# The attention mask moved from matmuls to accumulating transfers, and the row biases to GpSimd and ScalarE

## What is computed

```python
x = rotate_pairs(x, theta[b], phi[b])
h = gelu(x @ Wi[e] + bi[e]); x = ln(x + h @ Wo[e] + bo[e]) * gamma[e] + beta[e]      # e = expert of b, 256 -> 1024 -> 256
out = gelu(x @ w1 + b1) @ w2 + b2                                                   # c = 0, 1: "narrow"
out = gelu(gelu(x @ w1_sr + b1_sr) @ w2_sr + b2_sr) @ w3_sr + b3_sr                 # c = 2: "deep", 256 -> 512 -> 256 -> 256
x = ln(x + out) * gamma2 + beta2
x = adaptive_ln(x, timestep[b])
scores = q @ k.T / 4 + fside[b, head];  scores[mask[b]] = -inf                      # 16 heads of 16 columns
x = x + (softmax(scores) @ v) @ Wo + bo
x = x + gelu2(ln(x) * g2 + beta2 @ W1 + b1) @ W2 + b2                               # gelu2(h) = h * sigmoid(1.702 h)
```

## Time and profile before

| | before |
|---|---|
| three runs | 2249.8, 2251.36, 2251.6 us (median 2251.36) |
| the profiled execution, its own time | 2250.72 us |
| its span | 2248.9 us |
| TensorE busy | 2024.3 us, 90% |
| VectorE busy | 1563.6 us, 70% |
| ScalarE busy | 1314.8 us, 58% |
| GpSimd busy | 122.6 us, 5% |
| share of the 16 DMA engines taken by SyncE's queue | 50.3% |

### The profile page before, as it was taken

How to read it: one execution, slowest core, us unless ns; L and a number is a source line. 1 busy time by engine, 2 the same in 40 slices (tenths; PEclk the granted TensorE clock), 3 DMA queues, 4 the chain that set the end, 5 groups by cost and what they waited for, 6 DMA issues and landing times.

```text
span 2248.9 us, 43734 instructions
## 1 busy us (share of the span) xinstructions
PE 2024.3 (90%) x14735; PEld 1739.7 (77%) x14735; DVE 1563.6 (70%) x5410; ACT 1314.8 (58%) x2086; POOL 122.6 (5%) x268
## 2 busy tenths in 40 slices
PE   4488999999999999999999999999999999998986
PEld 3467788888878888878788777888787788877865
DVE  4357777777776677776776777766777767777763
ACT  3256566656556666556666656665665666565632
POOL 1000000000000000000000000000000000000000
PEclk8689999999999999999999999999999999999998
DMA  5355554555455455555554455455555545554440
GB/s 195 101 158 158 166 155 141 168 180 161 148 167 151 146 175 162 166 166 151 145 168 157 153 158 181 139 159 171 170 159 168 171 128 170 176 163 144 124 137 24
DMA packets 217606, 347.52 MB, mean 155 GB/s; under 512 B 29139, under 2 KB 115443, under 8 KB 217364
## 3 DMA queue, kind: packets, MB, share of 16 engines
q1 hardware_dynamic: 217364, 344.37, 50.3%
HBM read 285.51 MB, written 58.79 MB: 153 GB/s over the span
## 4 chain that ended last, share of the span: by engine, by line
PE 62%; DVE 11%; DMA 9%; SPq 6%; issue 6%; ACT 5%; DVEq 0%; ACTq 0%; POOL 0%; POOLq 0%
PE pD L425 41%; DMA out<-res 8%; PE pX L640 8%; PE pS L425 7%; SPq L267 5%; DVE x_scores L1131 3%; PE pC L425 3%; PE pD L430 2%; ACT gelu_out L737 2%; DVE x_scores L917 2%; DVE res L920 2%; ACT hid L737 1%; PE pC L660 1%; DVE res L914 1%; DVE xc_lo L914 1%
## 5 line engine op out<-in xcount | busy, mean ns | idle before, releaser
L1131 DVE CUSTOM_DVE_ANT_0 x_scores<-pS,bias_ring 128x256 f32<-128x256 f32 x1024 | 390.8, 419 | 221.6 <-PE pS L425 207.5
L737 ACT ACT_TABLE_LOAD x347 | 445.2, 1283 | 34.7 <-PE pD L425 28.1
L737 ACT ACTIVATE probs<-pX 128x512 f32<-128x512 f32 x512 | 304.8, 595 | 257.1 <-PE pX L640 252.3
L640 PE MATMUL pX<-ident,x_scores 128*128 128x128 f32 x2048 | 326.9, 283 | 60.2 <-DVE x_scores L917 58.4
L640 PEld LDWEIGHTS pX<-ident,x_scores 128*128 128x128 f32 x2048 | 237.7, 143 | 129.6 <-DVE x_scores L917 97.8
L917 DVE TENSOR_SCALAR x_scores<-x_scores,row_max 128x256 f32<-128x256 f32 x1024 | 315.5, 351 | 18.3
L425 PE MATMUL pS<-k_stack,q_stack 96*128 96x256 f32 x1024 | 306.1, 381 | 0.0
L425 PE MATMUL pD<-x,raw 128*128 128x256 f32 x1024 | 244.0, 381 | 3.6 <-ACT gelu_out L737 2.9
L425 PE MATMUL pD<-raw,gelu_out 128*128 128x256 f32 x1024 | 241.6, 379 | 0.0
L425 PEld LDWEIGHTS pS<-k_stack,q_stack 96*128 96x128 f32 x1024 | 199.7, 195 | 23.4
L425 PEld LDWEIGHTS pD<-raw,gelu_out 128*128 128x128 f32 x1024 | 189.9, 190 | 23.5
(11 more groups left out here) (152 smaller groups left out, 3691.7 us busy)
## 6 DMA issues: line engine op xcount, KB each, us to landing
bias_ring<-in_fside SPq DMA_DIRECT2D x512, 256.0 KB, 3.2
raw<-in_experts SPq DMA_DIRECT2D x128, 512.0 KB, 6.6
q_spill<-hid SPq DMA_DIRECT2D x96, 256.0 KB, 3.4
k_spill<-hid SPq DMA_DIRECT2D x96, 256.0 KB, 3.4
q_stack<-q_spill SPq DMA_DIRECT2D x128, 192.0 KB, 3.2
k_stack<-k_spill SPq DMA_DIRECT2D x64, 384.0 KB, 5.4
x_nat<-in_x SPq DMA_DIRECT2D x32, 256.0 KB, 7.6
norm<-in_expert_rows SPq DMA_DIRECT2D x32, 256.0 KB, 7.5
```

Source lines behind the costliest of these rows:

```text
L640: last = e.transpose(pX[:, k, t * P:(t + 1) * P], x_scores[:, u % NX, t, k * P:(k + 1) * P], ident[:, :])
L737: return e.activation(o, i, func, bias=bias, scale=scale)
L1131: e.tensor_tensor_reduce(x_scores[:, xn, t, :], pS[:, t, :], bias_ring[:, n, t, :], 1.0, -3.4e38, ALU.add, ALU.max, row_max[:, xn, t:t + 1 ...
```

## The change

Six parts, all in one diff.

1. The mask matmul goes. `mask_add` becomes f32 in one buffer, made by ScalarE after all transfers of the batch element before have landed. GpSimd issues, for each head, a transfer that adds `mask_add` to the head's slot of `bias_ring` in place; VectorE waits for that one (`dma_masked`).
2. `bias_ring` gets 7 slots and holds bias, sum and scores alike; `x_scores` goes. A slot is free once TensorE has turned it, so `load_bias(u)` waits for `turned` of head u - 7.
3. `open_bank` goes. GpSimd adds the rows of bias to the residual in SBUF instead (`biased`, 128 x 512, four for each b), after TensorE has turned the same tile. bv goes through Wo once at the start and is part of the row of bo (`dve_folded`).
4. ScalarE writes b1 into the bank (`seed`, 128 x 512 into PSUM) before each `hidden` step. g2 is multiplied into W1 and beta2 into b1 at the start, so the affine step after the last norm is a plain copy.
5. The row of the branch's bias is loaded for each b; the staging of weights has 5 places instead of 6.
6. `ORDER` and `SKIP` are new for all five engines.

```diff
-    "PE": "gfhghhrghhghhfghhghhhhgghhghhrrhhhfhhhfrfrhhrfhhfhrhhrhhhrhhrrhhfrhfhh",
+    "PE": "hhhfrhhfhrhfhrhhrhhfhrrhhrfhhhhhhhhfhhffrghhghhhghhhgrghhrgghhgrhhgh",
...
-SKIP = {"PE": (2, 56, 27), "ACT": (4, 33, 28), "DVE": (5, 31, 32), "POOL": (0, 0, 2), "SP": (3, 20, 3)}
+SKIP = {"PE": (12, 106, 41), "ACT": (13, 55, 54), "DVE": (12, 50, 46), "POOL": (4, 38, 6), "SP": (8, 38, 4)}
...
-        NBIAS, NX, NPROBS = 4, 4, 5
+
+        NBIAS, NPROBS = 7, 5
...
                 if u >= NBIAS:
-                    e.wait_ge(sem["max_made"], 2 * (u - NBIAS) + 2)
+                    e.wait_ge(sem["turned"], u - NBIAS + 1)
...
-            def open_bank(n, sel):
-
-                mm(pD[:, n, :, :], sel.to_broadcast([P, P]), bias_rows[:, :].unsqueeze(1).to_broadcast([P, T, H]), start=True)
...
-                    mm(pS[:, :, :], eye_bf[:, :], mask_add[:, b % 2, :, :], True, False)
                     for t in range(T):
-                        last = mm(pS[:, t, :], q_stack[:, g, par, t * P:(t + 1) * P], k_stack[:, g, :], False, True)
+                        last = mm(pS[:, t, :], q_stack[:, g, par, t * P:(t + 1) * P], k_stack[:, g, :], t == 0, t == T - 1)
...
-                    for n in range(2):
-                        mm(pD[:, TAIL, n, :], bias_rows[:, n * P:(n + 1) * P],
-                           hid_sel[:, m2:m2 + 1].to_broadcast([P, S]), start=n == 0)
-                    to_turned(TAIL, "W1", FF, 2 * P * m2, xc_parts, (sem["x3_lo"], b + 1), start=False).then_inc(sem["w1"], 1)
+                    e.wait_ge(sem["x3_lo"], b + 1)
+                    e.wait_ge(sem["hid_seeded"], 4 * b + m2 + 1)
+                    to_turned(TAIL, "W1", FF, 2 * P * m2, xc_parts, start=False).then_inc(sem["w1"], 1)
...
+                e.wait_ge(sem["dma_mask"], 16 * (b + 1))
+                if b:
+                    for n in range(NBIAS):
+                        e.wait_ge(sem[f"dma_masked{n}"], 16 * ((b * NH - n + NBIAS - 1) // NBIAS))
+                act(flat(mask_add[:, :, :]), flat(mask_u8[:, :, :]), ACT.Copy, scale=MASKED).then_inc(sem["mask_made"], 1)
...
+                    act(pD[:, TAIL, :, :], cols[:, col_at["L3_cond_b1"] + 2 * m2:col_at["L3_cond_b1"] + 2 * m2 + 2]
+                        .unsqueeze(2).to_broadcast([P, 2, S]), ACT.Copy).then_inc(sem["hid_seeded"], 1)
...
+            def biased(rows, bias, name):
+                e.tensor_tensor(rows[:, :, :], rows[:, :, :], bias.unsqueeze(1).to_broadcast([P, T, H]), ALU.add).then_inc(sem[name], 1)
...
+                for u in range(NH * b, NH * b + NH if b < NB else 0):
+                    n = u % NBIAS
+                    e.wait_ge(sem["mask_made"], b + 1)
+                    e.wait_ge(sem[f"dma_bias{n}"], 16 * (u // NBIAS + 1))
+                    e.dma_start(flat(bias_ring[:, n, :, :]), flat(mask_add[:, :, :]),
+                                accum_op=ALU.add).then_inc(sem[f"dma_masked{n}"], 16)
+                    yield
```

More of the change, by code:

```diff
@@ L206, in slots @@
         def slots(tile):
-            return [flat(tile[:, 2 * n:2 * n + 2, :, :].rearrange("p a b c -> p a (b c)")) for n in range(2)]
-        staging = [*slots(x_scores), *slots(probs), *slots(bias_ring)]
+            return [flat(tile[:, n:n + 2, :, :].rearrange("p a b c -> p a (b c)")) for n in range(0, tile.shape[1] - 1, 2)]
+        staging = [*slots(probs), *(slots(bias_ring)[n] for n in (2, 0, 1))]
         NSTAGE = len(staging)
-        R_BRANCH, R_O, R_FF, R_V, R_HID = E, E + 3, E + 4, E + 5, E + 6
         def col(name, n=0):
@@ L356, in weights @@
                 e.wait_ge(sem["dve_w"], runs_before(NSTAGE * PIECE))
-                for u in range(NBIAS):
+                for u in range(4):
                     load_bias(u)
@@ L362, in weights @@
                 load_norm3(0)
+                yield
+                for i in (9, 10):
+                    piece(i)
+                yield
+                e.wait_ge(sem["dve_w"], runs_before(NW))
+                for u in range(4, NBIAS):
+                    load_bias(u)
                 yield
@@ L450, in to_turned, with to_natural @@
                 return last
-            def to_natural(bank, wt, first, ins, low_ready=None, start=False):
+            def to_natural(bank, wt, first, ins, low_ready=None, start=True):
                 hi, lo = W[wt]
@@ L502, in wide_in, with wide_out @@
                     last.then_inc(sem["wide_in"], 1)
-                def open_wide():
-                    if not b:
-                        e.wait_ge(sem["pool_set"], 5)
-                        e.wait_ge(sem["dve_sel"], 1)
-                        e.wait_ge(sem["dve_rows"], 1)
-                    if b:
+                def wide_out(m2):
+                    if m2 == 0 and b:
                         e.wait_ge(sem["dve_sum2"], T * b)
-                    open_bank(SUM_F, select[:, 0, b:b + 1])
-                def wide_out(m2):
                     e.wait_ge(sem["wide_gelu"], 8 * b + 2 * m2 + 2)
@@ L527, in wide @@
                 yield
-                open_wide()
                 wide_out(0)
@@ L753, in weights @@
                     yield
-            def affine_T(bank, buf, scales, shifts, hi, aff, b):
-                for k in range(K):
-                    act(buf[:, k, :], pD[:, bank, k, :], ACT.Identity, bias=shifts[k], scale=scales[k]).then_inc(sem[aff + "_aff"], 1)
-                e.wait_ge(sem[aff + "_aff"], 2 * (b + 1))
-                act(flat(hi[:, :, :]), flat(buf), ACT.Copy).then_inc(sem[aff + "_hi"], 1)
             def wide(b):
@@ L874, in tail, with seed @@
                 e.wait_ge(sem["ffn_turned"], b + 1)
-                if b:
-                    e.wait_ge(sem["ffn_lo"], 4 * b - 1)
-                affine_T(TAIL, gated[:, 0, :, :], [col("L3_cond_g2", k) for k in range(K)],
-                         [col("L3_cond_beta2", k) for k in range(K)], xc_hi, "x3", b)
+                act(flat(xc_hi[:, :, :]), flat(pD[:, TAIL, :, :]), ACT.Copy).then_inc(sem["x3_hi"], 1)
                 yield
+                def seed(m2):
+                    if m2 == 0:
+                        e.wait_ge(sem["x3_lo"], b + 1)
+                    else:
+                        e.wait_ge(sem["gated"], 4 * b + m2)
+                    if not b and m2 == 0:
+                        e.wait_ge(sem["dve_folded"], 1)
+                    act(pD[:, TAIL, :, :], cols[:, col_at["L3_cond_b1"] + 2 * m2:col_at["L3_cond_b1"] + 2 * m2 + 2]
+                        .unsqueeze(2).to_broadcast([P, 2, S]), ACT.Copy).then_inc(sem["hid_seeded"], 1)
                 def tanh(m2):
@@ L893, in high @@
                     act(flat(ffn[:, m2 % 2, 0, :, :]), flat(gated[:, m2 % 2, :, :]), ACT.Copy).then_inc(sem["ffn_hi"], 1)
+                seed(0)
+                yield
                 for m2 in range(NM):
@@ L897, in tail @@
                     yield
+                    if m2 + 1 < NM:
+                        seed(m2 + 1)
+                        yield
                     high(m2)
@@ L1227, in front @@
             def front(b):
+                e.wait_ge(sem["y1_turned"], b + 1)
+                e.wait_ge(sem["dma_brow"], 16 * (b + 1))
+                biased(y_nat, branch_row[:, :], "y1_biased")
+                yield
                 for i in range(2):
@@ L1281, in layouts @@
     e, h, ff = wi.shape
-    rows = cat([v["L1_cond_bo"], *(v[n].reshape(-1, h) for n in ROWS_OF)])
-    sels = np.zeros((P, 7), np.float32)
-    for n in range(7):
-        sels[[e + 3 + n, NROWS + e + 3 + n], n] = 1.0
     return {
```

236 lines of the change are left out of this document (117 added, 119 removed), and 3 rows, old and new, of the table SEMAPHORES.

## The result

The changed kernel takes **2349.6 us** (median; its runs 2331.6 to 2350.6) against 2251.5 us for the kernel before beside it: ratio 1.0414, 95% interval 1.0362 to 1.0466. It is 98 us slower. The forecast was 2160 us, and the range up to 2300 us does not hold the result.

The account below looks back on a forecast made before the run. TensorE was taken to bound the steady part. From 2250.7 us, -175 (TensorE's work), -50 (x2), +58 (turns), +62 (bias through two queues) and +15 (start) made -90, so 2161, given as 2160 us; range 2075 to 2300 us.

Parts of the forecast that it names:

- mask matmuls gone: TensorE's scores without the mask matmul, 0.21 us less for each of 512 heads: -108 us.
- bias matmuls: TensorE without the 64 + 96 `open_bank` matmuls, -37 us, and the 256 matmuls of b1, -30 us.
- x2: TensorE's wait for the tile `res`, 57.4 us, mostly gone because the output is issued behind fewer loads: -50 us.
- turns: TensorE's turns close behind their scores: six of 16 heads with too little work between instead of five, +58 us.
- GpSimd's 128 row additions: GpSimd's 128 adds and 512 issues, under 20 us a cycle, priced at 0.
- bias through two queues: Bias loaded by SyncE, then masked by GpSimd's transfer; VectorE stands still where SyncE is held up: +62 us.
- What lies beside other work: Added work on ScalarE (seeds, mask steps), GpSimd and VectorE, said to be covered by TensorE: near nothing, 0.
- rival 2: Masked bias comes late and the kernel is slower: 2302 us, or 2440 if a second place waits as long; chance 0.19.
- second place: First heads after k is spilled: last loads behind six spills, ScalarE's mask waiting for all 16 transfers; 2440 us.
- first place: VectorE's wait at head 3, or 6 in deep cycles: +62 us, 4.4 us more a cycle in the slower rival.
- It decides from 6.0 us to landing on: Threshold for the masking transfer's landing time from which the slower rival decides (3.2 + 90 / 32).
- What would show it: Signs: TensorE busy near 1850 us, `bias_ring` wait up some 60, `res` wait under 10; wrong if DMA share above 85%.

Follow-up runs that it names:

- e9: The kernel before without its 512 mask matmuls (the mask is left out of the result), nothing else changed: 2208.7 us, ratio 0.9817.
- e6: The changed kernel without masking transfers and with GpSimd's four row additions shrunk to one column each: 2162.1 us, ratio 0.9603.
- e2: The changed kernel without its masking transfers, VectorE waiting for the bias load itself, mask left out of the result: 2199.6 us, ratio 0.9765.
- e1: The changed kernel with two mask buffers in turn instead of one: 2231.9 us, ratio 0.9932.
- e5: The changed kernel, single mask buffer, with SyncE issuing the last three bias loads ahead of q's and k's spills instead of behind: 2260.2 us, ratio 1.0034.
- e12: The changed kernel with two mask buffers, branch steps reordered, late bias loads ahead of spills, and GpSimd's 128 row additions each in two halves: 2183.1 us, ratio 0.9685.
- e3: The changed kernel with masking transfers as plain copies instead of additions, so the result lacks the bias: 2239.9 us, ratio 0.9944.
- e7: The changed kernel with two mask buffers and two steps around the branch reordered, on TensorE and VectorE: 2178.4 us, ratio 0.9673.
- e10: The kernel before with masking transfers, two mask buffers, a ring of 8, no mask matmul, and SyncE's order fitted to them: 2202.3 us, ratio 0.9777.
- e8: The kernel before with masking transfers, two mask buffers, a ring of 8, no mask matmul; only GpSimd's order changed: 2423.5 us, ratio 1.0750.

## Why the prediction was wrong

The forecast was a gain of 90 us, the result a loss of 98. The runs split the way from 2251.5 to 2349.6 us. Each row is a difference of two medians, so it holds to a few us. e9 has the orders of before and e6 those of the change, so the second row holds all that the new orders, the ring and the seeds do; no run takes it apart.

| step | forecast | measured | from |
|---|---|---|---|
| mask matmuls gone | -108 | -43 | before to e9 |
| bias matmuls (-67), x2 (-50), turns (+58), start (+15) | -44 | -47 | e9 to e6 |
| GpSimd's 128 row additions | 0 | +38 | e6 to e2 |
| bias through two queues: transfers, two buffers | +62 | +32 | e2 to e1 |
| one mask buffer | 0 | +118 | e1 to after |
| sum | -90 | +98 | |

**The step that failed most** is in "What lies beside other work": 32 mask steps on ScalarE, "All in all that is near nothing". I priced the step by its duration and gave its wait to VectorE in rival 2, at a chance of 0.19. The wait is ScalarE's own: it must see all 16 additions landed before it overwrites the only buffer, and `xa_hi` and the exponentials are queued behind it. 68.9 us of direct wait cost 118: TensorE's wait for `xa_hi` behind it, 75.3 us, goes to 0.7 with the second buffer, and the granted clock of 1000 to 2000 us goes from 0.95 to 0.99. This is rival 2's second place, "the last loads of a batch element stand behind six spills and ScalarE's mask waits for all 16 transfers"; the mechanism stood there, and the e5 run confirms the place. Its price there was an extra 4.4 us a cycle on top of the first place's, 2440 in all; measured were 3.7 us a cycle.

**Bias through two queues.** The first place, VectorE waiting at head 3 or 6, hardly opened: 3.5 us in the whole run, not 62. And this though the terms were priced too low: the issue at 0.7 us against 1.08 measured, the addition's landing at 3.2 against 4.9, the load's at 3.2 against 4.7. By the trace the masked block of head 3 lands 6.0 us before its maxima start and that of head 6 2.3 us before (means of batch elements 6 to 29), so VectorE asks later than the sum took it to. The +32 that stands in this row in place of the 62 comes by another way: from e2 to e1 the subtraction's mean goes from 397 to 416 ns and TensorE's waits for `bias_ring` and `hid` grow by 23.8 and 6.4 us. That is read from the waits and not shown by a run of its own. "It decides from 6.0 us to landing on" was the wrong test, since it looked at the median of one transfer; what decided was the last of a burst, 8.8 us. The Trainium skill ("Collectives: The Full Stack", The bandwidth ceiling) has an adding transfer at half the rate of a copy; the trace agrees, 33.3% against 16.3% of the queues' time. I had this rule and its 93%, and a share of 0.93 to 0.95 came in the fast kernels as well: a full queue was no proof of a slow kernel.

**The mask matmuls.** -108 was right as work (97 measured) and wrong as time. The words "all of it on the engine that bounds" took TensorE to be the only bound, though its idle time is made of many short waits, for which each matmul is the cover. I asked of the turns alone what covers them, and of no other wait.

**The second row** came out by luck, through errors that cancel. TensorE's waits for `hid` (94 us together) came with the new order and were not in the sum. The waits for `xc_hi` and `gated`, which I had at 0, went away with b1's matmuls (33.3 and 22.7 us in e9; together under 1 in e6), x2 gave 66 instead of 50, and the turns' wait grew from 72.3 to 101.1 us, 29 and not 58. The start's +15 was not measured by itself.

**GpSimd's additions at 0.** I asked only whether GpSimd had time. It had, at 31% busy. The additions hold VectorE up: at 1029.33 us two subtractions take 2.13 us while this ran on GpSimd:

```profile
1029.72 1.58 POOL L1229 TENSOR_TENSOR y_nat<-y_nat,branch_row 128x512 f32<-128x512 f32 x1
```

The Trainium skill ("SBUF — State Buffer", SBUF: two separate sides) says that VectorE and GpSimd share a pair of ports as an exclusive lock, held for a whole instruction. The runs agree in kind: mean 351 ns with no 128x512 addition, 397 with 128, 595 with 640. By that rule half an instruction should hold VectorE up for less, and e12 agrees where additions alone run: 822 ns at most against 1445. The 2349 ns beside an addition and an issue together are longer than one instruction explains, since half an addition takes 0.7 us.

**What would show it** named TensorE at 1850 us (1920.4 here, 1867.0 with two buffers, 1852.3 in e6), the turn's wait grown by 60 (by 94, from 58.4 to 152.8), and a DMA share above 85% as a sign of being wrong (0.87). Nearly all of the 94 comes in four steps: 14 with the mask matmul gone (e9), 29 from there to e6, 26 with the row additions (e2) and 24 with the transfers (e1). The wait for res under 10 us came true. Two slips changed nothing: a cycle by the sum is 66.9 - 90 / 32 = 64.1 us, not 64.5, and VectorE's 79% was taken of 61.5.

## What to carry to other kernels

Price a step that overwrites a buffer by the latest reader it waits for and by what is queued behind it on its engine, not by its duration. Ask this of every buffer that transfers read. Removing work from the busiest engine gives back only what did not cover another engine's latency: here 42.5 of 97 us. And when a change alters what a load waits for, go through the order of the queue that issues it again; the same transfers gave 2423 or 2202 us.

## What the runs showed of the hardware

- An accumulating transfer of 256 KB within SBUF (after, against e3's copy): 144 packets against 80, twice the queue time, 1083 ns against 558 ns of GpSimd to issue, 4.9 us against 3.4 to landing (medians); the shortest 3.3 against 2.2.
- Queues at a share of 0.94, 239 GB/s, carried the kernel of 2178 us (e7) with VectorE waiting for masked blocks 9.7 us in all.
- VectorE's 128x256 subtraction takes 344 to 356 ns undisturbed (e6) and up to 1445 beside GpSimd's 128x512 additions (e2). GpSimd's 512 issues alone do little: a mean of 358 and 360 ns, at most 516 (e10, e8). Beside both it reaches 2.1 us, and 2.3 with the additions in halves (e12). The maxima, which read PSUM as well, keep a mean of 418 to 420 ns in every run.
- GpSimd's addition to `y_nat`, which follows an issue, takes 1557 ns (median) with the change and 1264 where nothing is issued (e2).
